# A recommender tower in fp32: layer 2 runs five units behind layer 1 instead of six

## What is computed

```python
e = jnp.stack([tbl_0[ids[:, 0]], ..., tbl_31[ids[:, 31]]], axis=1)   # (2048, 32, 16)
x0 = xk = e
outs = []
for W in (W0, W1, W2):                       # W0 (32, 32, 64), W1 and W2 (32, 64, 64)
    xk = jax.nn.relu(jnp.einsum('bmd,bhd,mhk->bkd', x0, xk, W))
    outs.append(jnp.sum(xk, axis=2))
h = jnp.concatenate(outs + [dense_ctx], axis=1)          # (2048, 208)
h = jnp.maximum(h @ W_top1 + b_top1, 0.0)                # 512
h = jnp.maximum(h @ W_top2 + b_top2, 0.0)                # 256
y = h @ W_top3
```

## Time and profile before

| | us |
|---|---|
| runs of the kernel before | 1229.69, 1235.33, 1238.95 |
| the profiled execution | 1226.33 |
| its span | 1224.5 |
| TensorE (PE) busy | 1205.7 |
| VectorE (DVE) busy | 1154.4 |
| ScalarE (ACT) busy | 530.0 |
| GpSimd (POOL) busy | 671.2 |

### The profile page before, as it was taken

How to read it: one execution, slowest core, us unless ns; L and a number is a source line. 1 busy time by engine, 2 the same in 40 slices (tenths; PEclk the granted TensorE clock), 3 DMA queues, 4 the chain that set the end, 5 groups by cost and what they waited for, 6 DMA issues and landing times.

```text
span 1224.5 us, 17076 instructions
## 1 busy us (share of the span) xinstructions
PE 1205.7 (98%) x6598; PEld 634.3 (52%) x6598; DVE 1154.4 (94%) x557; ACT 530.0 (43%) x801; POOL 671.2 (55%) x689
## 2 busy tenths in 40 slices
PE   6999999999999999999999999999999999999998
PEld 6433444445555555555555555555555555555365
DVE  5789999999999999999999999999999999999994
ACT  3744434454443444444443443444444444444321
POOL 7757676767586565737556474655747541220202
PEclk7999999999999999999999999999999999999999
DMA  6799999999888899999999999899989998877740
GB/s 161 187 250 240 229 232 252 248 252 252 241 229 243 244 234 233 241 229 237 242 248 242 235 245 240 230 237 226 259 240 235 235 247 232 236 242 226 229 139 1
DMA packets 73531, 278.53 MB, mean 227 GB/s; under 512 B 29574, under 2 KB 38304, under 8 KB 41195
## 3 DMA queue, kind: packets, MB, share of 16 engines
q1 hardware_dynamic: 54936, 269.15, 83.2%
q0 software_dynamic: 15872, 4.09, 3.5%
q10 hardware_dynamic: 2642, 4.20, 1.4%
HBM read 273.16 MB, written 4.20 MB: 227 GB/s over the span
## 4 chain that ended last, share of the span: by engine, by line
PE 93%; DVE 3%; issue 1%; DMA 1%; POOL 1%; ACT 1%; SPq 0%; DVEq 0%; ACTq 0%
PE accs L907 69%; PE l0w L861 11%; PE l0w L828 4%; DVE prod L763 2%; PE xe L938 2%; PE xe L916 2%; PE l0w L811 1%; POOL emb L362 1%; DMA kept<-x_rows 1%; PE l0w L835 0%; PE accs L903 0%; DMA emb<-in_tbl,idx 0%; PE xe L948 0%; PE l0w L976 0%; DMA idx<-in_ids 0%
## 5 line engine op out<-in xcount | busy, mean ns | idle before, releaser
L907 PE MATMUL accs<-prod,w2s 128*64 128x512 f32 x2016 | 933.3, 594 | 0.7 <-DVE prod L763 0.5
L907 PE MATMUL accs<-prod,w1s 128*64 128x512 f32 x2016 | 928.3, 593 | 0.0
L763 DVE TENSOR_TENSOR prod<-kept,xe 128x2048 f32<-128x2048 f32 x256 | 583.8, 2281 | 34.9 <-PE accs L907 30.4
L763 DVE TENSOR_TENSOR prod<-kept,xp 128x2048 f32<-128x2048 f32 x256 | 583.0, 2279 | 7.2 <-ACT xp L532 7.2
L362 POOL DMA_INDIRECT emb<-in_tbl,idx x496 | 472.7, 953 | 194.1 <-issue 113.1
L907 PEld LDWEIGHTS accs<-prod,w1s 128*64 128x64 f32 x2016 | 272.7, 137 | 321.4 <-issue 200.1
L907 PEld LDWEIGHTS accs<-prod,w2s 128*64 128x64 f32 x2016 | 268.4, 137 | 52.1 <-issue 30.3
L518 ACT ACTIVATE sq<-l0w 128x1024 f32<-128x1024 f32 (+1 forms) x155 | 145.7, 940 | 170.9 <-PE l0w L828 80.8
L861 PE MATMUL l0w<-sq,u 128*64 128x512 f32 x640 | 200.9, 593 | 0.3 <-ACT sq L488 0.3
L401 POOL TENSOR_TENSOR x3f<-x3f 64x512 f32<-64x512 f32 x31 | 39.7, 1281 | 134.3 <-ACT x3f L568 134.0
L861 PEld LDWEIGHTS l0w<-sq,u 128*64 128x64 f32 x640 | 82.9, 137 | 55.8 <-issue 17.0
(11 more groups left out here) (108 smaller groups left out, 519.4 us busy)
## 6 DMA issues: line engine op xcount, KB each, us to landing
kept<-x_rows SPq DMA_DIRECT2D x252, 512.0 KB, 5.2
kept<-x_rows SPq DMA_DIRECT2D x504, 256.0 KB, 6.4
emb<-in_tbl,idx POOLq DMA_INDIRECT x496, 4.2
x_rows<-x3f ACTq DMA_DIRECT2D x31, 128.0 KB
kept<-in_small SPq DMA_DIRECT2D x1, 562.5 KB
kept<-in_small SPq DMA_DIRECT2D x1, 546.9 KB
prod<-in_w_all SPq DMA_DIRECT2D x1, 512.0 KB, 6.8
w1s<-in_w SPq DMA_DIRECT2D x4, 128.0 KB
```

The costliest lines, as they stand in the source:

```text
L763: nc.vector.tensor_tensor(prod[layer][:, q % BUFS[layer], :, :], kept[:, q % KEPT, :, :], xp[layer][:, :].unsqueeze(1).to_broadcast([128, ...
L907: last = mm(accs[64 * (layer - 1):64 * layer, s % 2, :], wk[layer][:, t, :], prod[layer][:, q % BUFS[layer], i, :], start=t == 0, stop=t = ...
```

## The change

`OFF` is 5 instead of 6:

```diff
-OFF = 6
+OFF = 5
 LAST = UNITS + OFF
```

## The result

The changed kernel takes 1242.43 us in the median of 8 runs (1241.11 to 1244.41), the kernel before, on the same chips, 1230.49 us in the median of 8 (1226.68 to 1238.95). The ratio is 1.010, with a 95% interval of 1.0075 to 1.0124: slower by 1%. The forecast was 1250 us, +14.5 us, range 1232 to 1262. The measured difference is +11.9 us.

What follows compares the result with a forecast made beforehand. The prediction took TensorE as the bound with VectorE close behind; 19.4 us of odd stalls less 3.4 us of drain and 1.5 us of early stalls gave +14.5 us on 1235.33, so 1250 us, range 1232 to 1262.

Steps and rivals of the forecast that it cites:

- The odd stall: VectorE's product needing an odd block's x2 is 0.81 us late; all of it reaches TensorE, making the period 37.09 us.
- How many: Periods where an output-layer piece makes TensorE's step end late: 24 x 0.81 = +19.4 us.
- The even stall: An even block's x2 is 0.84 us late, hidden in VectorE's 1.11 us of waiting for TensorE.
- the third rival: Even blocks' stalls count too, on top of the odd ones: +34.7 us, 1270 us; chance 0.11.
- the upper bound: Stalls over the 24 periods if the even ones count too: 24 x (0.81 + 0.84) = +39.6 us.
- The second rival: TensorE's first half goes on while its second waits, winning part back: +4.8 us, 1240 us; chance 0.14.
- The ends: The drain saves 3.4 us with one step less; layer 2's earlier start adds no cost.
- Drain: One step of layer 2 alone goes at the program's end, if the last products keep up: -3.4 us.
- Early stalls: VectorE's early waits for x2 behind other ScalarE work, 0.84 us at 134.05 and 0.72 us at 152.44, go: -1.5 us.
- The start: Layer 2 begins one step sooner, at step 5; the product gained falls into a 3.30 us wait: no cost.
- The sum: Whole program: 19.4 - 3.4 - 1.5 = +14.5 us, giving 1250 us, +1.2%.

Runs made afterwards that it cites:

- experiment 1: Changed kernel with the 24 output-layer pieces that stood in the last step of each eight moved one step later: 1225.48 us, ratio 0.9939 to the kernel before.
- experiment 3: Changed kernel with the same 24 output-layer pieces moved one step earlier: 1247.2 us, ratio 1.0127 to the kernel before.
- the second trace: Changed kernel run again with no edit, for a second trace: 1241.23 us.
- experiment 6: Changed kernel with two more evictions (1.15 us) in front of x2 of every even block but the first: 1242.49 us.
- experiment 9: Changed kernel with each load of kept waiting for one layer 2 product more: 1244.85 us, ratio 1.0118 to the kernel before.
- experiment 4: Changed kernel with one more eviction of 0.57 us in front of x2 of every odd block: 1262.28 us, ratio 1.0254 to the kernel before.
- experiment 5: Changed kernel with one more eviction of 0.57 us in front of x2 of every even block but the first: 1241.58 us.

## Why the prediction was right, point by point

**The odd stall.** Worked out as 0.81 us late and shown as such: the eviction starts 0.62 us after the last layer 1 matmul of step 119, and VectorE 0.03 us after its end. (The idle time before the product reads 0.73 us, since products that run back to back start 2.20 us apart at a length of 2.29: 0.73 + 0.09 = 0.82.) Rows of TensorE and one of ScalarE in the changed kernel's trace, at the end of step 119 and at the start of step 123:

```profile
589.29 0.59 PE L907 MATMUL accs<-prod,w1s 128*64 128x512 f32 x1
...
589.91 1.15 ACT L551 ACTIVATE xe<-accs 64x512 f32<-64x512 f32 x2 [0.46 <-PE accs L907]
...
601.31 0.59 PE L907 MATMUL accs<-prod,w1s 128*64 128x512 f32 x1
601.32 0.59 PE L907 MATMUL accs<-prod,w2s 128*64 128x512 f32 x1
601.74 0.59 PE L907 MATMUL accs<-prod,w1s 128*64 128x512 f32 x1
602.23 0.64 PE L907 MATMUL accs<-prod,w2s 128*64 128x512 f32 x1
602.33 0.61 PE L861 MATMUL l0w<-sq,u 128*64 128x512 f32 x1
602.71 0.59 PE L907 MATMUL accs<-prod,w2s 128*64 128x512 f32 x1
```

589.91 + 1.15 + 0.03 = 591.09. Step 123's second half starts at 602.23; the sum gives 591.09 + 8.79 + 2.28 + 0.05 = 602.21. The period was forecast at 37.09 us and is 37.10. That the stall comes from TensorE's work between two releases is shown by experiments 1 and 3 together.

**How many.** 24 periods by 0.81 us, +19.4 us; the trace has +19.78 us between steps 47 and 247, of which 19.71 us are in the 24 periods. There is a 25th odd stall that the forecast didn't have, 0.73 us at 1149.46. The piece in step 238 stands just ahead of the step whose end that x2 waits for, as all do in experiment 3. It costs 0.07 us: the wait for TensorE behind it has shrunk from 1.68 to 1.00 us, so this one stall is absorbed. The periods without pieces are 35.4 us as before (139.04, 174.46, 209.87 in the second trace).

**The even stall.** That it costs nothing was right. Its size was 0.55 us late (0.46 of idle time and 0.09 of spacing), not 0.84. While layer 2's half of the array waits at step 123, layer 1's half goes on (its two passes of the first contraction start at 601.31 and 601.74 above, layer 2's at 602.23 and 602.71), so step 123's last layer 1 matmul stands 4.86 us behind that 602.23 (at 607.09), where the earlier trace rows have 5.49 us (634.62 behind 629.13). ScalarE then starts x2 only at 608.05, behind a piece's result (L576, 0.39 us from 607.64). That VectorE waits for L551 some 36 us in total, as forecast, was in part luck: 34.7 us are 25 odd waits of 0.73 us, 24 even ones of 0.46 or 0.55 us in place of 0.75, and 4.4 us at the two ends that the forecast left out.

The forecast held, but **one step of the prediction failed, the price of the third rival**: it added the even stalls to the odd ones, 24 x (0.81 + 0.84). Experiment 6 shows that the two stand in the same slack. One and a half microseconds of even wait leave the period at 37.10 us. For even stalls of that size the upper bound should have been that of the odd stalls, 19.4 us, and the rival's 0.11 was too much.

**The second rival**, a part won back by the half that goes on, is refuted: it goes on, and the period is 0.82 us longer all the same. VectorE's release at 618.59 comes from layer 2's half (a matmul of w2s at 617.96), and at the turn the halves are together again (624.18 and 624.19 us, last section). The prediction also read the lead of the first half before as 0.1 us and no more; the pass behind it starts at 629.46 us in the first half and at 629.61 us in the second, 0.15 us apart, and that lead lasts on as well.

**The ends.** Drain: forecast -3.4 us, trace -3.34. VectorE's first product of the last block starts at 1220.22, behind a wait for x2 of 3.02 us. Layer 2's last matmul of step 255 starts at 1218.59, and 0.63 us later, at 1219.22, VectorE would have been free to go: the x2 wait decides by 1.0 us, as the forecast had it. Early stalls: forecast -1.5 us, trace -1.19 from the first product to step 47. The waits at 134.05 and 152.44 are gone, and VectorE meets TensorE a little earlier instead, 0.16 us at 140.40: together -1.37 us. The start, forecast at no cost, costs the other 0.18 us: x2 of block 0 is now waited for, 1.39 us at 59.52, and the wait of 3.30 us is gone for it.

**The sum.** From the first product on, the traces differ by 19.78 - 1.19 - 3.34 = +15.25 us, where +14.5 was forecast. The medians differ by 11.9 us, and in the two later pairs of measurements by 8.5 and 12.3 us (ratios 1.0075 and 1.0115). The fastest runs of all measurements differ by 1239.33 - 1225.42 = +13.9 us. What the medians lack may be in the spread: in the first eight runs each the kernel before spreads over 12 us and the changed one over 3, but later the changed one goes up to 1254. Traces of long runs put a large part of such a surplus on loads of kept that are late, with OFF = 6 and with OFF = 5. Whether the changed kernel has it less often stays open: experiment 9 took the loads' lead back and changed nothing that six runs can tell. The forecast of 1250 us was 7.6 us too high, since it took as base a median of three runs, 1235.33, which became 1230.49 with eight, 4.8 us less (that the base was off is chance, not a step of the working); the rest, rounding aside, is the difference of 14.5 and 11.9.

**Where the loss came from.** The two banks of accs take turns before and after the change, and no row of TensorE waits for L551 in either trace. The loss came by way of VectorE, which waits 34.7 us for L551 and whose queue held four products behind the one that waited: behind 591.09 they start at 593.30, 595.50, 597.70 and 599.89 us, about 2.20 apart, and the last of them is the one that step 123's second half waits for (599.89 + 2.28 = 602.17, against 602.23).

## What to carry to other kernels

Where two engines are both as busy as here (98% and 94% before), look for the loops of waits through a period and count each as its own path: what one engine is released by, what it must do, and what it releases. Here a delay added to the period only on the loop that was the longest (0.60 us in experiment 4, nothing in experiment 5), and two delays in one slack didn't add (37.10 us in experiment 6 as without it). Pulling a consumer forward by one step turned an eviction that had cover into a wait here (1.6 us of waits before, 34.7 after); before it is given up for that, see whether other work of the producer can be moved behind the point that is now late, as the output pieces could here: the same change, 1% slower, becomes 0.5% faster.

## What the runs showed of the hardware that was not expected

The fp32 contractions of the two layers run side by side, each on its half (128*64 in their rows): at 624.18 and 624.19 us (rows below) a pass of each starts, 0.64 us long. A half whose product was late did not hold the other at once. In step 123 layer 2's first pass starts at 602.23 us, 0.92 us behind layer 1's of the same contraction (601.31), and layer 1's second one has started in between, at 601.74. But the next instruction behind it in the program, L861, starts on layer 1's half only at 602.33 us, 0.10 us behind layer 2's pass and 0.59 us behind 601.74, where 601.31 and 601.74 are 0.43 us apart. From there on the lead is 0.79 us: the next passes of L907 start at 603.21 (layer 1) and 604.00 (layer 2). It lasts for tens of matmuls and ends at the next turn (L811), whose row has 128*128: the passes behind it start 0.01 us apart. The last contraction ahead of the turn, whose passes start at 621.89 and 622.32 us for layer 1 and at 622.68 and 623.11 us for layer 2:

```profile
621.89 0.59 PE L907 MATMUL accs<-prod,w1s 128*64 128x512 f32 x1
...
622.32 0.59 PE L907 MATMUL accs<-prod,w1s 128*64 128x512 f32 x1
622.68 1.02 PE L907 MATMUL accs<-prod,w2s 128*64 128x512 f32 x2
623.63 0.62 PE L811 MATMUL l0w<-ident_b,parts 128*128 128x128 bf16 x8
624.18 0.64 PE L907 MATMUL accs<-prod,w1s 128*64 128x512 f32 x1
624.19 0.64 PE L907 MATMUL accs<-prod,w2s 128*64 128x512 f32 x1
```

TensorE's busy time grew by most of what the odd stalls add: 1221.9 us against 1205.7 for the same 6598 matmuls, and 1201.7 us in experiment 1, where the odd stalls are gone. With longer stalls it grew by only a part: in experiment 4 it is 1230.5 us, 8.6 us more than in the changed kernel, for a span that is 17.3 us longer.
